# The last 25 slots of a software-pipelined kernel, rewritten as a closing program for each engine

## The chip, the cores and the metric

The kernel runs on one core of a Trainium2 chip. The core has TensorE (PE in the rows), VectorE (DVE), ScalarE (ACT), GpSimd (POOL) and SyncE (SP), which here only issues transfers. The metric is the device time of one execution in microseconds; the span is the part of it from the first to the last instruction.

## The reference

```python
def _L0_attn_ref(query, key_param, Wq, bq, Wk, bk, Wv, bv, Wo, bo):
    ...
    scores = jnp.einsum('blhe,bshe->bhls', queries, keys)
    A = sparsemax(scale * scores)
    out = jnp.einsum('bhls,bshd->blhd', A, values)
    out = jnp.transpose(out, (0, 2, 1, 3)).reshape(B, L, H * D)
    return out @ Wo + bo
def _L0_ffn_ref(x, Win, bin_, W1, b1, W2, b2, Wout, bout):
    s = jnp.einsum('btd,dm->btm', x, Win) + bin_
    h = jax.nn.relu(s[..., None] * W1 + b1)
    g = jnp.einsum('btmh,mh->btm', h, W2) + b2
    out = jnp.einsum('btm,md->btd', g, Wout) + bout
    return out
x = L0_attn_query
x = _layernorm(x + _L0_attn_ref(x, ...), axis=-1)
x = _layernorm(x + _L0_ffn_ref(x, ...), axis=-1)
```

x is 16 x 1024 x 512 in fp32. The attention has 16 heads and 32 key patterns; the feed-forward has 64 units s, each with 16 hinges relu(s * w1 + b1), summed with the weights W2.

## The kernel before, in words

The 16384 rows are 128 tiles of 128 rows (TILES). All engines run through one list of slots, 176 of them, numbered from 0. In slot n each engine does one step for several tiles at once, and the constants LAG_... say how many slots behind a tile is at each step: scores of tile n-1, the sparsemax in the next slots, the large product with the folded value and output weights of tile n-23 (LAG_WO, L663, four fp32 products of 512 columns), its residual with row sums on VectorE (n-24, L954), the first layernorm's result y (n-25), the transposes of y and the 64 units s (n-26, L648 and L677), the copy of s on ScalarE (n-27, L796), and so on. The scores of the last tile fall in slot 128 and the last large product in slot 150. From there to slot 175 the loop runs only the later steps.

The hinges are worked on in groups of four tiles (GROUP), 512 columns at a time. The 128 partitions hold the 64 units twice, once for each half of the 16 hinges, so a group takes 8 hinge steps: ScalarE writes one (L783) into one of two buffers `hinge`, and VectorE adds it times w2c into `acc` (L1111, then seven times L1115), two in a slot. When a group is full, its two halves are folded in the **group slot** (`split_lead`, slots 34, 38, ... 150 and then a last one in 156): ScalarE copies the upper half to `both` (L805), GpSimd adds the lower half (L512), ScalarE rounds the sum to `split` and `second` (L842, L843), and GpSimd writes the rest of the sum beside it (L514). Then TensorE can form the feed-forward output of the four tiles, one in a slot (n-34, L697 and L698; called f below). VectorE adds it to y (n-35, L954 again), and the second layernorm follows.

A layernorm is spread over three engines. GpSimd turns the row sum into two small numbers (L466, L468), ScalarE takes the sum of squares (L771), GpSimd makes the reciprocal root and the shift (L476, L481, L484), and one instruction on 128x512 applies them: for y in L831 or L1018, for the output in L825 or L1012. `vector_finishes` says who does that: ScalarE before slot 128 and VectorE from slot 128 on, together with the copy of the transposed y from PSUM (L855 on ScalarE, L1001 on VectorE). SyncE stores the output from the ring o_sb of four places (L423).

Every engine works strictly in the order of its code, and all waits are on semaphores. So an instruction that waits holds back everything behind it on its engine:

```python
                if lead is not None and lead != LAST:

                    pool.wait_ge(s_upper, lead // GROUP + 1)
                    nc.gpsimd.tensor_tensor(both[0:M, :], acc[0:M, :], both[0:M, :], ALU.add).then_inc(s_both, 1)
                    pool.wait_ge(s_hi, lead // GROUP + 1)
                    nc.gpsimd.tensor_tensor(split[M:P, :], both[0:M, :], split[0:M, :].bitcast(F32),
                                            ALU.subtract).then_inc(s_lo, 1)
```

## Time and profile before

| what | value |
|---|---|
| median of 3 runs | 1354.32 us (1354.13 to 1356.15) |
| the profiled execution | 1352.76 us, of which the span is 1351.0 us |
| mean granted TensorE clock | 0.967 |
| PE, DVE, ACT, POOL busy | 1251.9, 1138.9, 1053.6, 703.2 us |
| slots 128 to 150 in the trace | 1152.1 us to about 1294 us |
| after that, to the end of the span | about 57 us |

The granted clock is 1.00 at 2.4 GHz and 0.50 at 1.2 GHz. In a timeline row stand the start, the length, the engine, the line, the operation and its tiles; in square brackets how long the engine was idle ahead of it and what it waited for. Matmuls in fp32 are recorded as two entries each, so four products read x8. An instruction's successor can start some 0.08 us before its own end.

### The profile page before, as it was taken

The page shows a single profiled execution, that of the slowest core. Times are in us where ns is not written, and L with a number is a line of the kernel's source. Part 1 is how long each engine was busy: PE and PEld are TensorE (multiplying, and loading weights), DVE is VectorE, ACT ScalarE, POOL GpSimd, SP SyncE. Part 2 cuts the span into 40 slices and gives each one's busy share as a digit, 9 for nine tenths or more (in the row PEclk, how much of TensorE's full clock was granted, in tenths as well). Part 3 has the DMA queues.
Part 4 walks back from the last instruction along what each step waited for, and adds up shares of the span by engine and source line. Part 5 has one row for each costly group of instructions (what it writes and reads, how often), then busy time and mean ns, then how long its engine had stood idle before and what let it go on. Part 6 is the DMA issues. An engine that isn't in the chain of part 4 may idle for free. (4 is left out here: it accounts for less than half of the span.)

```text
span 1351.0 us, 25359 instructions
## 1 busy us (share of the span) xinstructions
PE 1251.9 (93%) x5838; PEld 867.3 (64%) x5838; DVE 1138.9 (84%) x4573; ACT 1053.6 (78%) x2269; POOL 703.2 (52%) x1674
## 2 busy tenths in 40 slices
PE   7982889999999999999999999999999999899962
PEld 6651666766776776776776776776776777555541
DVE  3977788889999999999999999999998999876764
ACT  2671756688898888899898898888899899666654
POOL 1330333345565555555556555555555556567663
PEclk9995999999999999999999999999999999999975
DMA  6380786555655655655655655655655655668733
GB/s 189 93 210 26 193 231 208 179 171 182 215 189 197 219 192 191 219 193 191 218 192 193 218 192 192 219 196 189 217 195 190 217 196 182 210 231 296 251 94 70
DMA packets 92374, 258.36 MB, mean 191 GB/s; under 512 B 16259, under 2 KB 16259, under 8 KB 75814
## 3 DMA queue, kind: packets, MB, share of 16 engines
q1 hardware_dynamic: 92198, 256.52, 58.7%
q14 instruction: 128, 1.05, 0.3%
q8 instruction: 48, 0.79, 0.2%
HBM read 206.13 MB, written 50.33 MB: 190 GB/s over the span
## 5 line engine op out<-in xcount | busy, mean ns | idle before, releaser
L663 PE MATMUL bank<-G_sb,pT 128*128 128x512 f32 x1024 | 461.1, 593 | 1.9 <-ACT pT L758 1.8
L663 PEld LDWEIGHTS bank<-G_sb,pT 128*128 128x128 f32 x1024 | 185.0, 191 | 185.9 <-issue 183.4
L1077 DVE MAX8 top<-bank 128x8 f32<-128x32 f32 x2048 | 212.3, 179 | 44.5 <-issue 44.5
L466 POOL TENSOR_TENSOR shift_sq<-sum,per_row_sq 128x1 f32<-128x1 f32 x256 | 96.0, 375 | 265.7 <-DVE y_sb L954 263.2
L771 ACT ACTIVATE unread<-y_sb,shift_sq 128x512 bf16<-128x512 f32 x256 | 183.9, 718 | 51.8 <-POOL minus_mean L468 51.7
L1115 DVE SCALAR_TENSOR_TENSOR acc<-hinge,w2c,acc 128x512 f32<-128x512 f32 x224 | 167.4, 748 | 61.7 <-ACT hinge L783 58.3
L783 ACT ACTIVATE hinge<-s_sb,b1c,w1c 128x512 f32<-128x512 f32 x256 | 205.8, 807 | 0.2
L588 PE MATMUL bank<-A_hi,xT_hi 128*128 128x512 f32 x512 | 204.0, 399 | 0.0
L590 PE MATMUL bank<-A_hi,xT_lo 128*128 128x512 f32 x512 | 203.9, 398 | 0.0
L589 PE MATMUL bank<-A_lo,xT_hi 128*128 128x512 f32 x512 | 203.7, 398 | 0.0
L481 POOL TENSOR_TENSOR rstd<-ve,minus_half 128x1 f32<-128x1 f32 x256 | 164.8, 644 | 43.1 <-POOL ve L476 42.8
L677 PEld LDWEIGHTS bank<-yT,Win_sb 128*128 128x128 f32 x1024 | 136.2, 195 | 73.7 <-issue 55.2
L849 ACT CAST xT_hi<-bank 128x512 fp32r<-128x512 f32 x128 | 74.7, 583 | 133.0 <-PE bank L637 133.0
L954 DVE SCALAR_TENSOR_TENSOR y_sb<-bank,y_sb 128x512 f32<-128x512 f32 x256 | 169.2, 661 | 0.0
L677 PE MATMUL bank<-yT,Win_sb 128*128 128x128 f32 x1024 | 138.6, 279 | 11.1 <-DVE yT L1001 11.1
L491 POOL TENSOR_TENSOR side<-side 128x256 bf16<-128x256 bf16 x128 | 85.5, 668 | 117.6 <-ACT side L866 117.6
L589 PEld LDWEIGHTS bank<-A_lo,xT_hi 128*128 128x128 f32 x512 | 97.1, 190 | 23.7
L590 PEld LDWEIGHTS bank<-A_hi,xT_lo 128*128 128x128 f32 x512 | 97.0, 189 | 23.8
L588 PEld LDWEIGHTS bank<-A_hi,xT_hi 128*128 128x128 f32 x512 | 97.1, 190 | 22.3 <-issue 0.5
L602 PE MATMUL bank<-ident,u_sb 128*128 128x128 f32 x512 | 78.9, 278 | 32.8 <-DVEq L1070 26.2
L758 ACT ACTIVATE pT<-bank 128x512 f32<-128x512 f32 x128 | 76.7, 599 | 39.8 <-PE bank L602 36.8
L1040 DVE TENSOR_TENSOR xT_lo<-bank,xT_hi 128x512 fp32r<-128x512 f32 x128 | 87.6, 685 | 21.1 <-ACT xT_hi L849 20.9
(133 smaller groups left out, 2421.9 us busy)
## 6 DMA issues: line engine op xcount, KB each, us to landing
G_sb<-G_of_heads SPq DMA_DIRECT2D x128, 1024.0 KB, 5.4
x_sb<-in_L_attn_query_dram SPq DMA_DIRECT2D x128, 256.0 KB, 4.7
y_sb<-in_L_attn_query_dram SPq DMA_DIRECT2D x256, 128.0 KB, 5.4
out_dram<-o_sb SPq DMA_DIRECT2D x256, 128.0 KB, 4.7
G_of_heads<-y_sb SPq DMA_DIRECT2D x64, 256.0 KB, 3.8
y_sb<-in_L_attn_Wk_dram SPq DMA_DIRECT2D x1, 1024.0 KB, 5.7
y_sb<-in_L_attn_Wq_dram SPq DMA_DIRECT2D x1, 1024.0 KB, 8.2
y_sb<-in_L_attn_Wv_dram SPq DMA_DIRECT2D x1, 1024.0 KB
```

The lines of the kernel that those rows point to most:

```text
L466: nc.gpsimd.tensor_tensor(shift_sq[:, par:par + 1], total[:, par:par + 1], per_row_sq[:], ALU.mult).then_inc(s_mean, 1)
L481: nc.gpsimd.tensor_tensor(rstd[:, par:par + 1], ve[:], minus_half[:], ALU.pow).then_inc(s_rstd, 1)
L588: nc.tensor.matmul(ps[:], hi[:, c, :], w_hi[:, c, :], start=start and c == 0, stop=False)
L589: nc.tensor.matmul(ps[:], hi[:, c, :], w_lo[:, c, :], start=False, stop=False)
L590: mm = nc.tensor.matmul(ps[:], lo[:, c, :], w_hi[:, c, :], start=False, stop=(c == C - 1))
L663: mm = nc.tensor.matmul(o_ps[i % 2][:], pT[:, bass.ds(pair_place(turn, i) + (i % H * C + c) * P, P)], G_sb[:, i % GR, c, :], start=(c == 0 ...
L677: mm = nc.tensor.matmul(s_ps[:, 0:P], Win_sb[:, c, :], yT[:, c, :], start=(c == 0), stop=(c == C - 1))
L771: nc.scalar.activation(unread[:], y_sb[:, i % YR, :], ACT.Square, bias=shift_sq[:, i % 2:i % 2 + 1], scale=1.0 / D ** 0.5, accum_out=var[: ...
L783: nc.scalar.activation(hinge[:, k % HR, :], s_sb[:, g % 2, :], ACT.Relu, bias=b1c[:, k:k + 1], scale=w1c[:, k:k + 1]).then_inc(s_hinge, 1)
L954: nc.vector.scalar_tensor_tensor(rows, ps[:], 0.0, other, ALU.add, ALU.add, accum_out=total).then_inc(s_rows, 1)
L1077: mx = nc.vector.max(top8[:, h, :], z_ps[i % 2][:, h * S:(h + 1) * S])
L1115: nc.vector.scalar_tensor_tensor(acc[:], hinge[:, k % HR, :], w2c[:, k:k + 1], acc[:], ALU.mult, ALU.add).then_inc(s_acc, 1)
```

## The change

The loop now ends after slot 150 (SLOTS is 151). What the 25 remaining slots did is written out by hand at the end of each engine's program:

- Hinge sums of the last two groups (tiles 120 to 123 and 124 to 127, called group 0 and 1 of the closing). VectorE adds only the even hinges into acc. The odd ones go to TensorE: `unit_sum` multiplies a hinge buffer by `w2_rows`, a 128x64 matrix that holds w2 and folds both halves, and `add_acc` brings acc in by a product with `both_halves`. The sums are in a PSUM bank, where ScalarE rounds them (`round_sum`) and VectorE takes the rest (`rest_of_sum`). GpSimd builds the two matrices in slot 144.
- Second layernorm of the last 12 tiles, 116 to 127: row sums and squares have columns of their own (`sum_end`, `var_end`), GpSimd handles two tiles with each small instruction (`mean_pair`, `norm_pair`), the squares of tiles 116 to 121 are on VectorE and those of 122 to 127 on ScalarE.
- Output of tiles 115 to 127: written in place in y_sb and stored from there, 7 of them by GpSimd, 3 by VectorE, 3 by ScalarE.
- The f of tiles 116 on rotates over four PSUM banks (`f_place`).

Two things change inside the loop as well. In the group slots for tiles 100, 104, 108, 112 and 116 (slots 134 to 150, ON_VECTOR) the add and the subtract on 64x512 move from GpSimd to VectorE. And the copy of the transposed y stays on ScalarE to the end, while y and the output move to VectorE from slot 131 on instead of 128.

```diff
-        SLOTS = TILES + FILL * UNROLL
-
-        def slots(eng, slot):
-
-
-            for turn in range(SLOTS // UNROLL):
-                for j in range(UNROLL):
-                    slot(turn, j)
+        SLOTS = TILES + LAG_WO
...
-        def vector_finishes(turn):
-
-
-            return isinstance(turn, int) and turn >= TILES // UNROLL
+        def vector_finishes(turn, j):
+
+
+            return turn * UNROLL + j >= TILES + FILL
...
+        ENDING = (LAST - GROUP, LAST)
+        FIRST_END = SLOTS - LAG_NORM2
+        ON_VECTOR = LAST - 6 * GROUP
...
+            if i >= LAST - 2 * GROUP:
+                return (f_ps, uT_ps, o_ps[0], o_ps[1])[i % GROUP]
...
+        FINAL_P = list(range(FIRST_END - 1, FIRST_END + 6))
+        FINAL_V = [FIRST_END + 6, FIRST_END + 8, FIRST_END + 10]
+        FINAL_A = [FIRST_END + 7, FIRST_END + 9, FIRST_END + 11]
+        SQUARE_V = list(range(FIRST_END, FIRST_END + 6))
+        SQUARE_A = list(range(FIRST_END + 6, TILES))
...
-            if 0 <= lead < LAST:
-                return [(lead, 2 * q + half)]
-            if lead == LAST and 2 * q < GROUP:
-                return [(lead, 4 * q + 2 * half), (lead, 4 * q + 2 * half + 1)]
-            return []
+            return [(lead, 2 * q + half)] if 0 <= lead < ENDING[0] else []
...
+                if base + j == TILES + UNROLL:
+
+                    nc.gpsimd.tensor_tensor(both_halves[:], ident[:, 0:M], ident[:, M:P], ALU.add).then_inc(s_halves, 1)
+                    pool.wait_ge(s_halves, 1)
+                    pool.wait_ge(s_p, TILES)
+                    nc.gpsimd.tensor_tensor(w2_rows, both_halves[:].unsqueeze(1).broadcast_to([P, KH, M]),
+                                            w2c[:].unsqueeze(2).broadcast_to([P, KH, M]), ALU.mult).then_inc(s_w2rows, 1)
                 lead = split_lead(turn, j)
-                if lead is not None and lead != LAST:
+                if lead is not None and lead < ON_VECTOR:
...
+            def mean_pair(n):
+
+                cols = pair_cols(n)
+                pool.wait_ge(s_r2, FIRST_END + 2 * n + 2)
+                nc.gpsimd.tensor_tensor(shift_sq_end[:, cols], sum_end[:, cols], per_row_sq[:].broadcast_to([P, 2]),
+                                        ALU.mult).then_inc(s_mean_end, 1)
...
+            norm1(TILES - 2)
+            mean(TILES, (TILES - 1) % 2, s_r1, sum1, s_mean1, minus_mean1, shift_sq1, s_shift1)
+            i = FIRST_END - 1
+            norm(i + 1, i % 2, s_var2, var2, s_ve2, ve2, s_mean2, minus_mean2, s_rstd2, rstd2, s_shift2, shift2, s_final)
+            norm1(TILES - 1)
+            final_end(nc.gpsimd, FINAL_P[0], s_final_p)
+            mean_pair(0)
+            mean_pair(1)
+            norm_pair(0)
+            for i in FINAL_P[1:3]:
+                final_end(nc.gpsimd, i, s_final_p)
+            norm_pair(1)
+            for i in FINAL_P[3:5]:
+                final_end(nc.gpsimd, i, s_final_p)
+            mean_pair(2)
+            mean_pair(3)
+            norm_pair(2)
+            for i in FINAL_P[5:7]:
+                final_end(nc.gpsimd, i, s_final_p)
+            norm_pair(3)
+            mean_pair(4)
+            mean_pair(5)
+            norm_pair(4)
+            norm_pair(5)
...
+                if LAST - 2 * GROUP + 2 <= base + i < ENDING[0]:
+                    pe.wait_ge(s_r1, TILES - GROUP + i % GROUP + 1)
+                elif base + i >= ENDING[0]:
+                    pe.wait_ge(s_r2, base + i - 3)
...
+            def unit_sum(g, k):
+
+                pe.wait_ge(s_hinge, SUMS + g * KH + k + 1)
+                nc.tensor.matmul(end_sums(g), w2_rows[:, k, :], hinge[:, k % HR, :], start=(k == 1),
+                                 stop=(k == KH - 1)).then_inc(s_kmm, 1)
+
+            def add_acc(g):
+
+                pe.wait_ge(s_acc, SUMS + (g + 1) * KH // 2)
+                nc.tensor.matmul(end_sums(g), both_halves[:], acc[:], start=False, stop=False)
...
+            end = FIRST_END
+            units_t(*at(TILES - 3, LAG_YT))
+            feed_forward(*at(end + 1, LAG_OUT))
+            units(*at(TILES - 3, LAG_YT))
+            units_t(*at(TILES - 2, LAG_YT))
+            pe.wait_ge(s_u1, TILES)
+            pe.wait_ge(s_halves, 1)
+            pe.wait_ge(s_w2rows, 1)
+            unit_sum(0, 1)
+            units(*at(TILES - 2, LAG_YT))
+            feed_forward(*at(end + 2, LAG_OUT))
+            unit_sum(0, 3)
+            units_t(*at(TILES - 1, LAG_YT))
+            feed_forward(*at(end + 3, LAG_OUT))
+            unit_sum(0, 5)
+            units(*at(TILES - 1, LAG_YT))
+            add_acc(0)
+            unit_sum(0, 7)
+            unit_sum(1, 1)
+            feed_forward(*at(end + 4, LAG_OUT))
+            feed_forward(*at(end + 5, LAG_OUT))
+            unit_sum(1, 3)
+            feed_forward(*at(end + 6, LAG_OUT))
+            unit_sum(1, 5)
+            feed_forward(*at(end + 7, LAG_OUT))
+            add_acc(1)
+            unit_sum(1, 7)
+            for i in range(LAST, TILES):
+                feed_forward(*at(i, LAG_OUT))
...
+            def end_hinge(g, k):
+
+                n = g * KH + k
+                if k == 0:
+                    act.wait_ge(s_sc, ENDING[g] + GROUP)
+                if k % HR == 0:
+                    act.wait_ge(s_acc, SUMS + n // HR if n >= HR else SUMS - 1)
+                elif n >= HR:
+                    act.wait_ge(s_kmm, n // HR)
+                else:
+                    act.wait_ge(s_acc, SUMS)
+                nc.scalar.activation(hinge[:, k % HR, :], s_sb[:, ENDING[g] // GROUP % 2, :], ACT.Relu,
...
+            def round_sum(g):
+
+                parts, high = end_split[g]
+                act.wait_ge(s_kmm, (g + 1) * KH // 2)
+                act.wait_ge(s_ones, 2)
+                nc.scalar.copy(parts[0:M, :], end_sums(g)).then_inc(s_hi, 1)
+                act.wait_ge(s_hi, ENDING[g] // GROUP + 1)
+                nc.scalar.copy(high[0:M, :], parts[0:M, :].bitcast(F32)).then_inc(s_high, 1)
...
+            copy_s(LAST)
+            end_hinge(0, 0)
+            copy_yT(TILES - 3)
+            end_hinge(0, 1)
+            end_hinge(0, 2)
+            square(0, TILES - 1 + LAG_NORM1, LAG_NORM1, s_mean1, s_var2, FIRST_END, shift_sq1, s_ve1, var1, s_var1)
+            copy_s(LAST + 1)
+            end_hinge(0, 3)
+            copy_yT(TILES - 2)
+            end_hinge(0, 4)
+            copy_s(LAST + 2)
+            end_hinge(0, 5)
+            copy_yT(TILES - 1)
+            end_hinge(0, 6)
+            copy_s(LAST + 3)
+            end_hinge(0, 7)
+            end_hinge(1, 0)
+            end_hinge(1, 1)
+            round_sum(0)
+            for k in range(2, KH):
+                end_hinge(1, k)
+            round_sum(1)
+            for i in SQUARE_A:
+                square_end(i)
+            for i in FINAL_A:
+                final_end(act, i, s_final_a)
...
-                if split_lead(turn, j) == LAST:
-                    dve.wait_ge(s_upper, TILES // GROUP)
+                late = split_lead(turn, j)
+                if late is not None and late >= ON_VECTOR:
+                    dve.wait_ge(s_upper, late // GROUP + 1)
                     nc.vector.tensor_tensor(both[0:M, :], acc[0:M, :], both[0:M, :], ALU.add).then_inc(s_both, 1)
-                    dve.wait_ge(s_hi, TILES // GROUP)
-                    nc.vector.tensor_tensor(last_split[M:P, :], both[0:M, :], last_split[0:M, :].bitcast(F32),
-                                            ALU.subtract).then_inc(s_lo, 1)
-                if in_range(turn, j, LAG_YT) and vector_finishes(turn):
-                    i = j - LAG_YT
-                    dve.wait_ge(s_yT, base + i + 1)
-                    dve.wait_ge(s_s, base + i)
-                    dve.wait_ge(s_yTc, base + i)
-                    nc.vector.tensor_copy(yT[:].rearrange("p c n -> p (c n)"), ys_ps[:]).then_inc(s_yTc, 1)
...
+            end, last = FIRST_END, TILES - 1
+            residual_end(end)
+            make_y(last - 1)
+            residual(last + 1, o_ps[last % 2], s_o, y_sb[:, last % YR, :], s_xr[last % YR], 32 * (TILES // YR),
+                     y_sb[:, last % YR, :], sum1[:, last % 2:last % 2 + 1], s_mean1, s_r1)
+            add_hinge(0, 0)
+            residual_end(end + 1)
+            add_hinge(0, 2)
+            make_y(last)
+            add_hinge(0, 4)
+            residual_end(end + 2)
+            add_hinge(0, 6)
+            residual_end(end + 3)
+            rest_of_sum(0)
+            add_hinge(1, 0)
+            square_end(end)
+            square_end(end + 1)
+            add_hinge(1, 2)
+            square_end(end + 2)
+            square_end(end + 3)
+            residual_end(end + 4)
+            add_hinge(1, 4)
+            residual_end(end + 5)
+            residual_end(end + 6)
+            add_hinge(1, 6)
+            residual_end(end + 7)
+            rest_of_sum(1)
+            square_end(end + 4)
+            square_end(end + 5)
+            for i in range(LAST, TILES):
+                residual_end(i)
+            for i in FINAL_V:
+                final_end(dve, i, s_final_v)
```

On VectorE, the last group slot of the loop (slot 150) and the start of what follows, before; `both` is the folded sum, `yT` the transposed y:

```order
L954 SCALAR_TENSOR_TENSOR y_sb,sum<-bank,y_sb 128x512
L1001 COPY yT<-bank 128x512
L954 SCALAR_TENSOR_TENSOR y_sb,sum<-bank,y_sb 128x512
L1012 TENSOR_SCALAR o_sb<-y_sb,rstd,shift 128x512
L1018 TENSOR_SCALAR y_sb<-y_sb,rstd,shift 128x512
L1111 TENSOR_SCALAR acc<-hinge,w2c,b2c 128x512
L1115 SCALAR_TENSOR_TENSOR acc<-hinge,w2c,acc 128x512
```

The same place now, and the first rows of the closing:

```order
L1189 SCALAR_TENSOR_TENSOR y_sb,sum<-bank,y_sb 128x512
L1235 TENSOR_TENSOR both<-acc,both 64x512
L1189 SCALAR_TENSOR_TENSOR y_sb,sum<-bank,y_sb 128x512
L1246 TENSOR_SCALAR o_sb<-y_sb,rstd,shift 128x512
L1250 TENSOR_TENSOR split<-both,split 64x512
L1196 TENSOR_SCALAR y_sb<-y_sb,rstd,shift 128x512
L1358 SCALAR_TENSOR_TENSOR y_sb,sum_end<-bank,y_sb 128x512
L1196 TENSOR_SCALAR y_sb<-y_sb,rstd,shift 128x512
L1189 SCALAR_TENSOR_TENSOR y_sb,sum<-bank,y_sb 128x512
L1379 TENSOR_SCALAR acc<-hinge,w2c,b2c 128x512
```

The copy of yT is gone from VectorE, `both` and `split` have come in, and the first hinge of tiles 120 to 123 stands two residuals and one y later than before.

On TensorE, the closing from the first units to the first f of tiles 120 to 123, now (L731 are the units, L716 the transposes, L754 and L755 an f, L861 `unit_sum`, L867 `add_acc`):

```order
L731 MATMUL bank<-yT,Win_sb 128x128 x4
L754 MATMUL bank<-Wout_hi,split 128x512
L755 MATMUL bank<-Wout_lo,second 128x512
L861 MATMUL bank<-hinge,u_sb 64x512
L716 MATMUL bank<-ident,y_sb 128x128 x4
L754 MATMUL bank<-Wout_hi,split 128x512
L755 MATMUL bank<-Wout_lo,second 128x512
L861 MATMUL bank<-hinge,u_sb 64x512
L731 MATMUL bank<-yT,Win_sb 128x128 x4
L867 MATMUL bank<-acc,both_halves 64x512
L861 MATMUL bank<-hinge,u_sb 64x512 x2
L754 MATMUL bank<-Wout_hi,A_hi 128x512
```

The rows L861 and L867, fp32 products of 512 columns, are new; there are ten of them in the closing, and the units and transposes of the last tiles stand between them.

## Rows read from the trace of the kernel before

**Rows 1.** The page: span, and two lines of its 40 slices.
```profile
span 1351.0 us, 25359 instructions
...
PE   7982889999999999999999999999999999899962
...
PEclk9995999999999999999999999999999999999975
```
**Rows 2.** Busy by stretch: us, PE, PEld, DVE, ACT, POOL busy (instructions), clock, DMA, GB/s.
```profile
1204.00:1225.00 21.00, 21.00 (x89) 12.72 (x88) 15.27 (x35) 13.33 (x28) 14.44 (x38) 1.00 0.78 254
1225.00:1248.00 23.00, 21.38 (x89) 12.59 (x88) 16.94 (x36) 13.87 (x31) 16.32 (x41) 1.00 0.88 300
...
1294.00:1316.00 22.00, 11.63 (x44) 9.13 (x44) 13.27 (x27) 13.29 (x28) 12.80 (x32) 0.68 0.24 54
1316.00:1330.00 14.00, 4.24 (x8) 2.16 (x8) 9.86 (x18) 9.45 (x16) 4.99 (x13) 0.50 0.09 20
1330.00:1351.00 21.00, 5.14 (x9) 2.01 (x8) 6.93 (x19) 5.38 (x14) 8.19 (x33) 0.50 0.45 100
```
**Rows 3.** Timeline of PE, slots 129 to 135: its waits.
```profile
1163.99 1.16 PE L677 MATMUL bank<-yT,Win_sb 128*128 128x128 f32 x8 [2.60 <-DVE yT L1001]
...
1165.35 0.77 PE L697 MATMUL bank<-Wout_hi,split 128*128 128x512 f32 x1
...
1179.61 1.16 PE L677 MATMUL bank<-yT,Win_sb 128*128 128x128 f32 x8 [1.02 <-DVE yT L1001]
...
1183.59 0.19 PE L628 MATMUL bank<-differs,ones_col 128*1 128x4 f32 x2 [2.36 <-DVE differs L970]
...
1203.57 3.70 PE L663 MATMUL bank<-G_sb,pT 128*128 128x512 f32 x8 [1.75 <-ACT pT L758]
```
**Rows 4.** Timeline of PE: large products of slots 139, 143, 147, and slot 150's f.
```profile
1224.57 3.60 PE L663 MATMUL bank<-G_sb,pT 128*128 128x512 f32 x8
...
1247.89 3.60 PE L663 MATMUL bank<-G_sb,pT 128*128 128x512 f32 x8
...
1271.14 3.60 PE L663 MATMUL bank<-G_sb,pT 128*128 128x512 f32 x8
...
1293.97 0.50 PE L697 MATMUL bank<-Wout_hi,split 128*128 128x512 f32 x1 [1.10 <-POOL split L514]
```
**Rows 5.** Timelines of ACT, POOL and DVE in the group slot 150.
```profile
1289.65 0.62 ACT L805 COPY both<-acc 64x512 f32<-64x512 f32 x1 [0.57 <-DVE acc L1115]
...
1290.67 1.26 POOL L512 TENSOR_TENSOR both<-acc,both 64x512 f32<-64x512 f32 x1
...
1292.66 1.26 POOL L514 TENSOR_TENSOR split<-both,split 64x512 fp32r<-64x512 f32 x1 [0.73 <-ACT split L842]
...
1295.91 0.54 DVE L1111 TENSOR_SCALAR acc<-hinge,w2c,b2c 128x512 f32<-128x512 f32 x1 [3.24 <-ACT hinge L783]
```
**Rows 6.** Groups by line and shape, 1204 to 1294 us: busy us, mean ns | idle before.
```profile
L783 ACT ACTIVATE hinge<-s_sb,b1c,w1c 128x512 f32<-128x512 f32 x30 | 24.0, 799 | 0.0
...
L954 DVE SCALAR_TENSOR_TENSOR y_sb<-bank,y_sb 128x512 f32<-128x512 f32 x32 | 21.8, 680 | 0.0
L771 ACT ACTIVATE unread<-y_sb,shift_sq 128x512 bf16<-128x512 f32 x30 | 21.5, 718 | 25.0 <-POOL minus_mean L468 25.0
...
L1115 DVE SCALAR_TENSOR_TENSOR acc<-hinge,w2c,acc 128x512 f32<-128x512 f32 x27 | 20.4, 754 | 13.1 <-ACT hinge L783 13.1
```
**Rows 7.** Timelines of PE, ACT, POOL and DVE after slot 150.
```profile
1299.34 2.08 PE L677 MATMUL bank<-yT,Win_sb 128*128 128x128 f32 x8 [4.20 <-DVE yT L1001]
...
1344.76 0.72 ACT L771 ACTIVATE unread<-y_sb,shift_sq 128x512 bf16<-128x512 f32 x1 [1.70 <-POOL minus_mean L468]
...
1346.08 0.55 POOL L481 TENSOR_TENSOR rstd<-ve,minus_half 128x1 f32<-128x1 f32 x1 [0.17 <-POOL ve L476]
...
1347.05 0.55 DVE L1012 TENSOR_SCALAR o_sb<-y_sb,rstd,shift 128x512 f32<-128x512 f32 x1 [1.97 <-POOL shift L484]
```
**Rows 8.** Two lines by source: ns least/median/most, first to last start.
```profile
L1033 DVE TENSOR_TENSOR u_sb<-u_raw,step x108: 691/692/1726, 196.3 to 1172.7; 128x512 f32<-128x512 f32 x108
...
L507 POOL MEMSET A_lo<- x1: 529/529/529, 1158.7 to 1158.7; 128x512 f32 x1
```

261 lines of the change are left out of this document (187 added, 74 removed).

## The prediction

> **What bounds the kernel now.** I read the page's slices first [rows 1]: PE is at 9 tenths or more almost everywhere, and falls only in the last two slices, where its clock falls too. The change lies in the last 200 us, so I read the windows there next [rows 2]. From 1204 to 1225 us PE is busy for all 21.00 us, four slots long. In 1225 to 1248 it is busy 21.38 of 23. From 1294 us on nobody is bound by his own work: in the last 21 us PE has 5.14 us, DVE 6.93, ACT 5.38 and POOL 8.19. That is a chain of waits. So there are three stretches with three limits, and I cost each by itself: A, slots 128 to 134; B, slots 135 to 150; C, all behind it.
>
> In A the timeline of PE shows what it waits for [rows 3]: 2.60, 1.02, 2.36 and 1.75 us, together 7.73, each time for VectorE or ScalarE. After the longest, the first matmul of an f takes 0.77 us, against 0.50 at 1293.97 [rows 3, 4]: the clock had fallen to 1.2 GHz for a moment.
>
> In B the large products of slots 135, 139, 143 and 147 start at 1203.57, 1224.57, 1247.89 and 1271.14 [rows 3, 4]. Four slots take 21.00 us (5.25 a slot, PE's own work), then 23.32 and 23.25. The difference is the group slot: ScalarE copies half of acc, GpSimd adds 64x512 in 1.26 us but only from 1290.67 on, since its norms stand ahead, ScalarE rounds, GpSimd subtracts in 1.26 us [rows 5]. f then waits 1.10 us for POOL [rows 4], and GpSimd's means are late, so ScalarE's squares are, so VectorE stands still for 3.24 us before the next hinge [rows 5].
>
> In C, from the f at 1293.97 to 1351.0, are 57.0 us. Here every tile goes around once: f, residual, mean, square, norm, output. In the last rounds a square starts at 1344.76 and its output at 1347.05, 2.29 us later, with 1.70 us of idle ScalarE ahead of the square [rows 7].
>
> **The change, part by part.**
>
> *A, slots 128 to 134.* In slots 128 to 130 VectorE loses the copy of yT, y and the output, three instructions of some 0.6 us a slot (as other 128x512 ones: 0.68 in L954, 0.55 in L1012 [rows 6, 7]). I count 0.6 + 0.5 + 0.5 = 1.6, and 0.7 of waiting once. VectorE is then early by 3.6 us at the end of slot 129. PE's wait of 2.60 for yT goes away, since ScalarE, which now copies it, is idle in that slot; with it goes about 1.3 us of slow clock, 3.9 in all. In slot 130 the new copy stands behind the rounding of the group and PE waits for it, +1.3. In slot 131 the wait of 1.02 goes, and in 132 VectorE's comparison is early, so that about half of the 2.36 goes (-1.2). In slot 134 the split is on VectorE, so ScalarE comes to its last pT sooner: half of 1.75 (-0.9). Sum: -3.9 + 1.3 - 1.0 - 1.2 - 0.9 = -5.7; I take -5.2. Bounds: -3 (only the 2.60 goes) to -7.7 (all four waits).
>
> *B, slots 135 to 150.* If every slot were PE's 5.25 us, the group waits give back 2.3, 2.25 and, from slot 147 to slot 150's f, 22.83 - (3 x 5.25 + 3.44 + 0.81) = 2.8. Here 3.44 is the row's 3.60 for four large products without the last one's tail of 0.16 [rows 4], and 0.81 is what then remains of 5.25 for the units of a tile beside an f (0.55) and transposes (0.45). Sum -7.4. Is there a ring that takes more than 5.25? One goes: residual on VectorE 0.68, means on POOL about 0.5, square 0.72, hinge 0.80, square 0.72, hinge 0.80, add on VectorE 0.75 [rows 6]: 4.97, and less with the overlaps. In a group slot the copy of acc, VectorE's add, two roundings and the copy of yT stand ahead of the squares: 0.6 each, some 6.6 us for that slot and 21.0 for four. That is what PE takes too, so nothing is left over there; hence -6.7 rather than -7.4. On POOL, slot 144 gets the making of w2_rows, a two-input product over 512 elements for which L512 is the nearest row (1.26 us, 512 elements), and a small one, 1.5 in all; ScalarE's squares wait for it, and PE has about half a slot in hand: +0.7. B is -6.0, bounds -3 to -7.4. Here VectorE has the group add and subtract, 1.4 us in a group slot, and is 3.24 us idle there now, so they cost nothing; without that cover they would cost their 1.4.
>
> So slot 150's f starts at 1293.97 - 11.2 = 1282.8.
>
> *C, the closing.* What is removed: 25 rounds of the loop, one mean and norm per tile in turn, and 8 of the 16 adds of a hinge (0.75 each). What is new: ten fp32 products of 512 columns on PE. Four of them are 3.60 us in the loop with the tail, 0.86 each without it [rows 4]. At 1.2 GHz they are 1.72, by the units, x8 in 2.08 us there [rows 7] against half of that in the loop. PE's list in C is 3 units and transposes (1.25 each), 12 f (0.55), ten products: 19 us at 2.4 GHz, and 37 at 1.2. DVE has some 21 us, ACT 23, POOL 17 to 23. Nobody is the bound at the high clock, so I follow the chain, with time 0 at slot 150's f, in pairs for the two clocks:
> - f 0.6, residual 0.7, y of tile 126 0.5, residual of 127 0.6, mean 0.5, ScalarE behind a hinge 1.1, square 0.7, norm and y of 127 1.6: 6.3 (6.7).
> - Meanwhile PE does the units of 126, f, one unit_sum, and the transposes of 127; they end at 8.7 (11.3). Then f, unit_sum, copy of yT, units of 127: 11.1 (15.7).
> - VectorE's fourth add, add_acc, hinge 7, unit_sum: 13.1 (19.1). Rounding, and its rest on VectorE, two hops: 15.1 (21.2).
> - Group 1: three even hinges with VectorE's squares and residuals in between, four unit_sums and three f on PE: 24.0 (32.5). Round and rest: 25.4 (33.9).
> - Two squares on VectorE 1.4, norm of a pair 1.3, two outputs on POOL 1.8, next norm 1.3, means: ScalarE starts the squares of 124 to 127 at 31.4 (39.9). Four squares 2.9, the last norm 1.3, an output 0.8: 36.6 (45.0).
> - From the last output to the end, as now, 1351.0 - 1347.6 = 3.4 [rows 7]: 40.0 (48.4).
>
> So C is -17.0 at full clock throughout and -8.6 at half throughout. In the stretch before, the clock fell once PE had stood idle for 4.20 us, and did not come back while PE was busy for some 80% [rows 2, 7]. My chain has PE idle for under 2 us at a time, but busy for only 19 of 26 us, so I expect it to fall for part of the closing: 44, plus 1 for what follows, 45. C is -12.0.
>
> The outputs of 512 columns on POOL are not in the trace. From below a memset of 512 columns, 0.53 us [rows 8], from above a two-input op of as many, 1.26 [rows 5]; with one tensor input it is nearest the middle, 0.9. Seven of them, four in the chain. The row of L1033 on VectorE, 0.69 us as a rule and 1.73 at most [rows 8], says that a VectorE instruction with two SBUF inputs is at times held, and POOL's folds run then. VectorE's hinge adds and squares have two SBUF inputs and meet POOL's outputs, each up to 1 us: I take one us in all; the upper bound is 5.
>
> The Trainium skill (SBUF — State Buffer, the section on two separate sides) makes a rule of this: such a VectorE instruction and a GpSimd one exclude each other for their whole length. It speaks against GpSimd's outputs; by it every meeting costs up to a full instruction, and the sum would be near that upper bound, 1334 in place of 1330 for the profiled execution. The same notes (GPSIMD Engine Reference, elementwise cycle accounting) have 769 ns for 512 elements in the best case, as an estimate 0.13 us less a tile than I took.
>
> **Sum.** -5.2 - 6.0 - 12.0 = -23.2, from the profiled execution's 1352.76: 1329.6. The median of the runs is 1.56 above that one, so I state 1331.
>
> **The rivals.**
> 1. The closing at full clock and POOL's outputs unhindered: C is -17.0, so 1324.6, 1326 beside the median. For it: the chain leaves no long idle time on PE. Against: PE's busy share there is below the loop's.
> 2. PE at 1.2 GHz through the closing, where ten products of 1.72 make it the bound, and VectorE and POOL hold each other: C is -8.6 + 5 = -3.6; 1352.76 - 14.8 = 1338.0, or 1339.5. By the exclusion rule of the skill named above this is where the time would go.
> 3. Slower than before. One mechanism: the copy of yT on ScalarE closes a ring, since it waits for PE's transposes, which wait for VectorE's y, and the squares and hinges now stand behind it. The ring is 4.97 + 0.6 by the rows above if nothing overlaps, 5.6 a slot, and the slots of B take 5.8 on average now. To eat the 17 to 18 us of C and A over 20 slots it would have to be 0.9 above today's, 6.7 a slot; at 7 the time would be near 1360. Against it: ScalarE is idle 25.0 us before its squares in 90 us [rows 6], more than the 9 us that 15 copies take.
> 4. The closing is shorter on paper only, each pair waiting for its second tile: then A and B alone remain and C is 0, 1341.6, or 1343.
>
> **How the numbers follow.** My forecast, a clock that falls for part of the closing (1327 to 1336), 0.55. Rival 1, 0.18. Rival 2, 0.19. Rival 4, 0.05, rival 3 or something like it 0.03. The range 1323 to 1341 takes in rivals 1 and 2, with A and B at their bounds partly. About 0.2% (2.7 us) is what a measurement of this kernel can tell from no change: faster 0.95, within it 0.02, slower 0.03.
>
> **What the profile after would show.** The f of slot 150 at 1281 to 1285 us. Large products of slots 139, 143 and 147 21 to 21.5 us apart, without a wait of f for POOL; PE without the 2.60 us idle time. In the closing, PE's clock between 0.5 and 1; unit_sum at 0.9 or 1.7 us; POOL's outputs at 0.8 to 1.3; from that f to the end 40 to 49 us. Wrong would be: groups still 23 us apart (another ring), a unit_sum that waits for its hinge for several us, or POOL's outputs at over 2 us.

## The result, and the profile after

The changed kernel takes 1333.66 us (median of 4 runs, 1332.68 to 1335.14), the kernel before 1354.22 in the same comparison: a ratio of 0.9856, 95% interval 0.9844 to 0.9868, 20.6 us less. A second comparison, beside the first three experiments, gives 1333.92 against 1355.61 (0.9846, 0.9833 to 0.9860). The forecast was 1331, with a range of 1323 to 1341.

The profiled execution has a span of 1333.0 us; it was the one that took 1335.14. The page, as in [rows 1]:

```profile
span 1333.0 us, 25293 instructions
...
PE   6982889999999999999999999999999999989993
...
PEclk9995989999999999999999999999999999999998
```

The second-last slice went from 6 to 9 tenths busy, and the clock is at full speed up to the last slice. In [rows 1] it had fallen to 7 and 5. The windows of the last 175 us show the same by stretch (columns as in [rows 2]):

```profile
1158.00:1200.00 42.00, 37.45 (x167) 23.14 (x165) 26.65 (x63) 34.21 (x74) 23.77 (x66) 0.96 0.70 230
...
1223.00:1245.00 22.00, 21.57 (x90) 12.94 (x89) 15.19 (x34) 16.27 (x35) 12.46 (x39) 1.00 0.86 278
...
1293.00:1303.00 10.00, 8.88 (x34) 3.76 (x34) 4.29 (x8) 6.66 (x11) 1.95 (x5) 1.00 0.12 26
1303.00:1313.00 10.00, 6.60 (x16) 2.11 (x16) 8.02 (x20) 4.89 (x7) 7.05 (x14) 1.00 0.25 56
1313.00:1323.00 10.00, 2.11 (x8) 1.42 (x8) 5.20 (x14) 4.88 (x13) 5.33 (x15) 0.85 0.58 128
1323.00:1333.00 10.00, 0.00 (x0) 0.00 (x0) 1.09 (x2) 3.00 (x5) 1.27 (x5) 0.50 0.60 132
```

The clock column is the thing to see: 1.00 while the closing's products run, although PE is busy for only 66% of the ten microseconds from 1303 on. It falls only behind PE's last product, which ends at 1316.1, and there it costs nothing.

PE's waits and large products, the counterpart of [rows 3, 4]:

```profile
1165.21 0.66 PE L766 MATMUL bank<-ident,u_sb 128*128 128x128 f32 x4 [1.04 <-ACT pT L931]
...
1170.55 1.16 PE L731 MATMUL bank<-yT,Win_sb 128*128 128x128 f32 x8 [1.25 <-ACT yT L961]
...
1179.96 0.19 PE L792 MATMUL bank<-differs,ones_col 128*1 128x4 f32 x2 [2.12 <-DVE differs L1212]
...
1180.97 4.89 PE L818 MATMUL bank<-G_sb,pT 128*128 128x512 f32 x8
...
1200.59 3.70 PE L818 MATMUL bank<-G_sb,pT 128*128 128x512 f32 x8 [0.74 <-ACT pT L931]
...
1222.67 3.70 PE L818 MATMUL bank<-G_sb,pT 128*128 128x512 f32 x8 [0.79 <-DMA G_sb<-G_of_heads]
...
1250.54 3.70 PE L818 MATMUL bank<-G_sb,pT 128*128 128x512 f32 x8 [0.78 <-DMA G_sb<-G_of_heads]
...
1286.96 0.48 PE L754 MATMUL bank<-Wout_hi,split 128*128 128x512 f32 x1
```

The 2.60 us wait for yT is gone, and with it the 1.02. In its place stand 1.04 for pT and the forecast 1.25 for a copy of yT that ScalarE makes late. The 2.36 is now 2.12, the 1.75 is 0.74. In slots 135 to 150 no wait for GpSimd is left; what ends PE's waits there is the transfer of G (the folded value and output weights that each large product reads, 1 MB a tile), four times, 2.42 us together. Before, none of PE's waits in these slots ended with it. The groups of four slots from 135, 139 and 143 take 22.08, 21.70 and 22.63 us; the forecast had 21 to 21.5, and another ring as the sign that it was wrong. The f of slot 150 has no wait at all (1.10 in [rows 4]).

Counted from slot 128's large product, which starts at 1152.13 before and 1152.67 after, the three stretches are, in microseconds:

| | before | after | forecast change | measured change |
|---|---|---|---|---|
| A, to slot 135's large product | 51.44 | 47.92 | -5.2 | -3.5 |
| B, from there to slot 150's f | 90.40 | 86.37 | -6.0 | -4.0 |
| C, the closing | 57.03 | 46.04 | -12.0 | -11.0 |

With the 0.54 by which this execution reached slot 128 later that makes the 18.0 between the two spans. The medians lie 20.6 apart.

Last, the end of the closing, as in [rows 7], from the timelines of ScalarE, DVE and SP's queue:

```profile
1320.24 0.72 ACT L1101 ACTIVATE unread<-y_sb,shift_sq_end 128x512 bf16<-128x512 f32 x1 [4.72 <-POOL minus_mean_end L606]
...
1323.68 2.32 ACT L307 ACTIVATE y_sb<-y_sb,shift_end,rstd_end 128x512 f32<-128x512 f32 x3
```
```profile
1325.19 0.55 DVE L309 TENSOR_SCALAR y_sb<-y_sb,rstd_end,shift_end 128x512 f32<-128x512 f32 x1 [1.27 <-POOL shift_end L625]
```
```profile
1324.51 6.24 SPq L473 DMA_DIRECT2D out_dram<-y_sb  x10
```

ScalarE waits 4.72 us before it can square tile 124, though VectorE had the residuals of 124 and 125 done 3.4 us earlier, at 1316.85: GpSimd makes the outputs of 120 and 121 and a norm first. The last output ends at 1326.0. The end is 7.0 us after it, where it was 3.4 before. SP issues the stores of the last five tiles one by one, 0.62 us each, up to 1330.75. It had stood at tile 123's, whose output waited for ScalarE's squares.

So three questions were open. Is B now held by G's transfers? Is the tail held by SP's issues or by the data? What does each part of the change give?

### The profile page after: what moved, and what is told of

It reads as the page before. It is cut to its first block and busy times, and to the rows that moved or that the text cites. A ratio compares the mean times of both kernels' runs of the same rounds, so it can differ in the third digit from the quotient of the medians.

```text
span 1333.0 us, 25293 instructions
## 1 busy us (share of the span) xinstructions
PE 1251.6 (94%) x5858; PEld 863.7 (65%) x5858; DVE 1120.3 (84%) x4545; ACT 1066.7 (80%) x2290; POOL 680.9 (51%) x1642
## 3 DMA queue, kind: packets, MB, share of 16 engines
q14 instruction: 128, 1.04, 0.3%
## 5 line engine op out<-in xcount | busy, mean ns | idle before, releaser
L1349 DVE SCALAR_TENSOR_TENSOR acc<-hinge,w2c,acc 128x512 f32<-128x512 f32 x210 | 156.4, 745 | 63.0 <-ACT hinge L971 61.7
L971 ACT ACTIVATE hinge<-s_sb,b1c,w1c 128x512 f32<-128x512 f32 x240 | 193.3, 808 | 0.0
L944 ACT ACTIVATE unread<-y_sb,shift_sq 128x512 bf16<-128x512 f32 x244 | 175.0, 717 | 6.9 <-POOL minus_mean L518 6.6
L731 PEld LDWEIGHTS bank<-yT,Win_sb 128*128 128x128 f32 x1024 | 134.1, 191 | 65.3 <-issue 58.6
L531 POOL TENSOR_TENSOR rstd<-ve,minus_half 128x1 f32<-128x1 f32 x244 | 153.8, 630 | 41.0 <-POOL ve L526 40.7
L1189 DVE SCALAR_TENSOR_TENSOR y_sb<-bank,y_sb 128x512 f32<-128x512 f32 x244 | 160.1, 660 | 1.8 <-PE bank L755 1.3
L731 PE MATMUL bank<-yT,Win_sb 128*128 128x128 f32 x1024 | 135.4, 275 | 3.0 <-ACT yT L961 3.0
```

Of the source, the lines that this page charges most:

```text
L531: nc.gpsimd.tensor_tensor(rstd[:, par:par + 1], ve[:], minus_half[:], ALU.pow).then_inc(s_rstd, 1)
L731: mm = nc.tensor.matmul(s_ps[:, 0:P], Win_sb[:, c, :], yT[:, c, :], start=(c == 0), stop=(c == C - 1))
L944: nc.scalar.activation(unread[:], y_sb[:, i % YR, :], ACT.Square, bias=shift_sq[:, i % 2:i % 2 + 1], scale=1.0 / D ** 0.5, accum_out=var[: ...
L971: nc.scalar.activation(hinge[:, k % HR, :], s_sb[:, g % 2, :], ACT.Relu, bias=b1c[:, k:k + 1], scale=w1c[:, k:k + 1]).then_inc(s_hinge, 1)
L1189: nc.vector.scalar_tensor_tensor(rows, ps[:], 0.0, other, ALU.add, ALU.add, accum_out=total).then_inc(s_rows, 1)
L1349: nc.vector.scalar_tensor_tensor(acc[:], hinge[:, k % HR, :], w2c[:, k:k + 1], acc[:], ALU.mult, ALU.add).then_inc(s_acc, 1)
```

## The experiments

Each was timed in 5 rounds beside the kernel before; ratios are to it. The changed kernel itself ran beside the first three experiments only. The intervals of most single experiments overlap with its 0.9844 to 0.9868 and 0.9833 to 0.9860, so their gains of one to three microseconds are not shown by the times alone. Because single profiles reach slot 128 at anything from 1149.4 to 1154.0 us, I compare stretches A, B and C, and they don't all repeat equally well:

- C of the closing as changed is 46.04, 46.05, 46.06 and 46.18 us in four executions of three programs, all with the group folds on VectorE. With the folds on GpSimd it is longer, 47.06, 47.63 and 49.25 (below).
- B of six executions with the same loop runs from 85.35 to 87.62 us, 86.37 on average. The spread is that of PE's waits for G, 1.27 to 3.70 us; without them B is 83.9 to 84.5.
- A has two values, 46.2 to 46.3 and 47.9 to 48.0 us (next part).

### The changed kernel again

> The changed kernel itself, as the yardstick for the three kernels that run beside it. All theories: ratio to the kernel before 0.985 to 0.987, about 1333.5 us, the f of slot 150 at some 1287 us in the profile and the closing 46.0 us.

Measured: 1333.92 us, 0.9846 (0.9833 to 0.9860). A 46.26, B 87.14, C 46.05. C repeats to 0.01 us. A is 1.66 shorter, and the difference is one thing: the large product behind the wait for differs takes 3.60 us here and not 4.89, and the transposes just ahead of it are shorter too. TensorE's clock had fallen there in the one execution and not in the other (called a slow product below).

### The group's add and subtract back on GpSimd

```diff
-        ON_VECTOR = LAST - 6 * GROUP
+        ON_VECTOR = LAST
```

> The changed kernel with the group's add and subtract back on GpSimd in the loop (ON_VECTOR = LAST); the closing is untouched. Theory 1 (stretch B gained because the group slot's stall for GpSimd went, and now the transfers of G hold it at 21.7 to 22.6 us per four slots): the group waits come back, f of a group waits about 1 us for GpSimd, four slots take 23.2 us, the f of slot 150 comes 3 to 4 us later, the time is 1336.5 to 1337.5. Rival a (the transfers of G set the pace of B in any case, and the gain in B came from the rest of the loop's change): four slots stay at 21.7 to 22.6 us, the time stays within 1 us of the changed kernel's. The closing takes 46 us in either.

Measured: 1336.70 us, 0.9865 (0.9849 to 0.9880), 2.8 us above the changed kernel beside it. B is 88.85, with 22.67 and 23.47 us for the four slots from 139 and from 143. The waits for G shrink to 0.36 us, and these come instead:

```profile
1264.56 1.16 PE L731 MATMUL bank<-yT,Win_sb 128*128 128x128 f32 x8 [2.24 <-ACT yT L961]
```

Theory 1 holds in size. Its wait stands elsewhere than I wrote: not f waits for GpSimd, but the units wait for a yT copy that is queued on ScalarE behind the rounding, and the rounding waits for GpSimd. The move to VectorE is worth about 2.8 us of the time. In the profile it shows in all three stretches: A is 47.30 without a slow product, 1.0 more than 46.26, and C is 47.06, 1.0 more, though the closing is the same program: its first unit_sum starts 4.6 us behind slot 150's f instead of 3.4. B without its waits for G is 88.5, against 83.9 to 84.5 in the changed kernel, so as an estimate the move frees some 4 us there and the transfers of G take about 2 of them back.

### The closing programs alone

```diff
-            return turn * UNROLL + j >= TILES + FILL
+            return turn * UNROLL + j >= TILES
-                if in_range(turn, j, LAG_YT):
+                if in_range(turn, j, LAG_YT) and not vector_finishes(turn, j):
                     copy_yT(base + j - LAG_YT)
```

VectorE copies yT in slots 128 to 150 again, where it did before, and ON_VECTOR is LAST.

> The closing programs alone: in the loop the yT copy, y and the output go back to VectorE from slot 128 on and the group's add and subtract back to GpSimd, as in the kernel before. Theory 1 (A gave 3 us, B 4, the closing 11): the f of slot 150 comes at 1293 to 1294.5 us, the closing takes 46 to 47 us, the time is 1340 to 1341.5, 7 us more than the changed kernel. Rival b (the loop's change is worth little by itself, the closing gives nearly all): less than 3 us more than the changed kernel, below 1336.5. Rival c (the closing only works since ScalarE and VectorE enter it early): the closing takes over 48 us and the time is above 1343.

Measured: 1346.76 us, 0.9938 (0.9924 to 0.9951). None of the three theories had all of this: it is 12.8 us above the changed kernel, where theory 1 had 7, and with the time of rival c the closing is not over 48 us. A is 53.27, B 92.55, C 47.63. The closing is nearly all there, 9.4 of 11.0 us. But the loop is longer than in the kernel before. In A it is chance: slots 128 to 134 are the program of the kernel before, and this execution has a slow product of 5.29 us behind the wait for differs, which the kernel before and the other execution of these slots (A 51.55, below) don't have. B is 2.15 us longer, most of it in the group that holds slot 144, 25.04 us against 23.25 in the kernel before; the waits for G are 1.90. The closing needs w2_rows, and GpSimd makes it there:

```profile
1258.47 0.32 POOL L561 TENSOR_TENSOR both_halves<-ident 128x64 f32<-128x64 f32 x1
1258.87 1.04 POOL L564 TENSOR_TENSOR u_sb<-both_halves,w2c 128x512 f32<-128x512 f32 x1
```

So the parts are not simply added: the closing's part costs something in the loop, and the loop's part takes it back. Against the changed kernel, which has a slow product too, A is 5.4 us longer here, B 6.2 and C 1.6. The loop's part without the closing was not run.

### Two tiles' stores from ScalarE's queue

```diff
+            for i in (125, 127):
+                act.wait_ge(s_final_a, FINAL_A.index(i) + 1)
+                for half in (1, 0):
+                    nc.scalar.dma_start(out_rows[i // H, i % H, half],
...
```

> The changed kernel with the stores of tiles 125 and 127 issued by ScalarE behind its last output, those of 123, 124 and 126 still by SP. In the changed kernel SP issues the last ten stores one after another in 6.24 us, from 1324.51 on, and the end comes 7.0 us after the last output. Theory 1 (the tail is the serial issue of stores, 0.62 us each): SP is through after six, at 1328.2, ScalarE after four behind 1326.0, at 1328.5, and the time falls by 2.2 to 2.6 us, to about 1331. Rival d (the tail is the transfer of the data and its landing): the time stays within 0.5 us of the changed kernel's, since the same bytes go out behind the same outputs.

SP leaves these two out. Measured: 1332.18 us, 0.9833 (0.9820 to 0.9846); the medians differ by 1.7, with overlapping intervals, the profiles' C by 1.2 (44.83). The two queues:

```profile
1321.45 3.84 SPq L475 DMA_DIRECT2D out_dram<-y_sb  x6
```
```profile
1322.16 3.05 ACTq L1135 DMA_DIRECT2D out_dram<-y_sb  x4
```

Both are through at 1325.2 us, 2.3 after the last output, as against 4.7 before: the issue got 2.4 shorter, as expected. The end still comes 3.4 us behind that, not 2.25. ScalarE's stores land after 3.5 us by the DMA view and the six of SP beside them after 2.9, where SP's alone took 2.4. So issue was the limit for half of the expected gain, then the landing takes over. Both theories are half right.

### All hinge adds on VectorE

```diff
-                nc.tensor.matmul(end_sums(g), both_halves[:], acc[:], start=False, stop=False)
+                nc.tensor.matmul(end_sums(g), both_halves[:], acc[:], start=True, stop=True).then_inc(s_kmm, 1)
```

The unit_sums go, and add_hinge is called for odd k too.

> The changed kernel with all eight hinge adds of each of the last two groups on VectorE again; TensorE only joins the halves of acc in one product a group. Seven to eight adds of 0.75 us come into VectorE's program, half of them on the chain from the f of slot 150 to the second rest. Theory 1 (the hinge sums set the chain in the middle of the closing, and sharing them is a main part of its gain): the closing takes 3 to 5 us more, 49 to 51 us, the time is 3 to 5 us above the changed kernel's, ratio 0.987 to 0.989. Rival e (VectorE's 12 us of idle time in the closing take the adds for nothing): within 1 us of the changed kernel's 0.985.

Measured: 1336.83 us, 0.9872 (0.9854 to 0.9890). C is 48.94, 2.9 more. The adds are only part of it. This is what else happened on PE:

```profile
1298.43 1.07 PE L867 MATMUL bank<-acc,both_halves 128*64 128x512 f32 x2 [1.95 <-DVE acc L1370]
1300.89 0.73 PE L754 MATMUL bank<-Wout_hi,A_hi 128*128 128x512 f32 x1 [1.39 <-DVE A_hi L1377]
1301.42 0.63 PE L755 MATMUL bank<-Wout_lo,A_lo 128*128 128x512 f32 x1
...
1312.70 1.97 PE L867 MATMUL bank<-acc,both_halves 128*64 128x512 f32 x2 [8.14 <-DVE acc L1370]
```

In the changed kernel a product of an f takes 0.40 us and the second add_acc 1.07. Here the clock has already fallen to 1.2 GHz at 1300.9, behind waits of 2.73, 0.56, 1.95 and 1.39 us in twelve, and it is low again behind the 8.14. The granted clock is 0.81 from 1296 to 1304 us, 0.71 from 1304 to 1312 and 0.50 from there. The unit_sums are work that VectorE needn't do, and they also keep PE's idle times below 1.6 us in the closing's middle, where the clock stays at 2.4 GHz. How the 2.9 us divide between the adds and the clock, this run doesn't separate.

### Statistics one tile at a time

```diff
+                for m in (2 * n, 2 * n + 1):
+                    cols = slice(m, m + 1)
```

around the bodies of mean_pair and norm_pair, each with its own wait.

> The changed kernel with mean and norm of the last twelve tiles one tile at a time, 1 column an instruction in place of 2, in the same places of GpSimd's program. That is 30 small instructions of 0.19 to 0.69 us more, some 9 us of GpSimd's time, about half of it while somebody waits for it. Theory 1 (pairs save GpSimd's time, and GpSimd's program is what the last rounds wait for): the closing takes 2 to 4 us more, ratio 0.9865 to 0.988. Rival f (a single tile's norm starts a square earlier, and this pays for the added instructions): within 1 us of the changed kernel's.

Measured: 1334.27 us, 0.9854 (0.9838 to 0.9870), which is no difference that this comparison can tell. In the profile the last output ends 41.9 us behind slot 150's f, 2.8 later than the 39.0 of the changed kernel, and C is 47.96, 1.9 longer; B was short in this execution (86.03). By this one profile the pairs save about 2 us of the closing, at the bottom of what I expected, and SP's queue hides a third of what they give; the times don't confirm it.

### The means of 124 and 125 earlier on GpSimd

```diff
             norm_pair(2)
+            mean_pair(4)
+            norm_pair(3)
+            mean_pair(5)
             for i in FINAL_P[5:7]:
                 final_end(nc.gpsimd, i, s_final_p)
-            norm_pair(3)
-            mean_pair(4)
-            mean_pair(5)
```

> The changed kernel with one change of order on GpSimd: after the norm of 120 and 121 come the means of 124 and 125, the norm of 122 and 123, the means of 126 and 127 and only then the outputs of 120 and 121. ScalarE's wait of 4.72 us before the square of 124 gets shorter by 2.0 to 2.5 us, since the residuals of 124 and 125 are done at 29.9 and 30.4 us behind the f of slot 150 and the square starts at 33.3. Theory 1 (SP's serial issue of stores sets the end): the last output comes 2 us sooner, but the stores of 120 to 127, 16 of 0.62 us, now start later than before, so the time stays within 0.7 us of the changed kernel's. Rival g (the chain of squares and norms sets the end): the time falls by 2.0 to 2.5 us, ratio 0.983.

Measured: 1332.93 us, 0.9841 (0.9827 to 0.9854); C 45.38, 0.7 less.

```profile
1316.24 0.72 ACT L1101 ACTIVATE unread<-y_sb,shift_sq_end 128x512 bf16<-128x512 f32 x1 [1.84 <-POOL minus_mean_end L606]
```
```profile
1318.72 10.25 SPq L473 DMA_DIRECT2D out_dram<-y_sb  x16
```

(The residuals that I put at 29.9 and 30.4 us are done at 29.3 and 29.9.) The wait falls from 4.72 to 1.84, the last output ends 37.2 us behind slot 150's f instead of 39.0, and the end moves by 0.7 only. SP now has sixteen stores in a row, 0.64 us each, from 1318.72 to 1328.97. Theory 1 holds. This is the clearest evidence on the tail: the chain gave 1.8 us and the queue of stores kept 1.1 of them.

### Four places for G

```diff
+        def G_place(i):
...
+            n = i % GR4 - GR
+            return pT[:, n * C * D:(n + 1) * C * D].rearrange("p (c n) -> p c n", c=C)
```

Tiles 112 to 127 take turns over the two places of G_sb and two in the half of pT that is free by then; each load waits for the product four tiles back.

> The changed kernel with four places in place of two for the G of the last sixteen tiles (two of them in the half of pT that is free then), loaded up to three tiles ahead; the same bytes. TensorE waited 2.4 to 3.2 us for G in slots 135 to 150. Theory 1 (a transfer lands too late only since it can't start before the place is free): the waits for G go, the slots are 5.25 us, from slot 135's large product to slot 150's f 84 to 84.5 us instead of 86.4 to 87.1, the time falls by 2.0 to 3.0 us. Rival h (the transfers are at the limit of what the DMA engines move, 0.87 to 0.91 busy): the waits are still there, merely later, and the time stays within 0.7 us.

Measured: 1332.63 us, 0.9834 (0.9821 to 0.9848). PE waits for G no more; B is 83.71, 2.7 less than the average of the six executions with two places and 1.6 less than the shortest, and the first two groups take 21.02 and 20.90 us. The DMA views of the changed kernel, from 1199 to 1283 us, then of this one, from 1201 to 1285, each starting a little before slot 135's large product (busy tenths of the DMA engines; what was moved):

```profile
DMA  8918989969898598699797998938989789998999
...
DMA packets 7207, 24.02 MB, mean 286 GB/s; under 512 B 1244, under 2 KB 1244, under 8 KB 5288
```
```profile
DMA  9999999999999988989989899998988998050500
...
DMA packets 7266, 24.02 MB, mean 286 GB/s; under 512 B 1264, under 2 KB 1264, under 8 KB 5360
```

The same 24 MB go through sooner, and the last slices of the second line are nearly empty. I read the digits 1, 5 and 3 in the first line as moments in which no place is free to load into. The limit in B was a missing place. The engines' bandwidth was not it.

### The copy of yT alone back on VectorE

```diff
-                if in_range(turn, j, LAG_YT):
+                if in_range(turn, j, LAG_YT) and base + j < TILES:
                     copy_yT(base + j - LAG_YT)
+                if in_range(turn, j, LAG_YT) and base + j >= TILES:
...
+                    nc.vector.tensor_copy(yT[:].rearrange("p c n -> p (c n)"), ys_ps[:]).then_inc(s_yTc, 1)
```

> The changed kernel with the copy of yT alone back on VectorE in slots 128 to 150. Closing programs alone stood 12.8 us above the changed kernel, the same with the early outputs and the yT copy on ScalarE (group folds still on GpSimd) only 2.8, so these two are worth 10 us together. Theory 1 (in A it is the 2.60 us wait for yT that goes with the copy, 4 us with the slow clock; in B VectorE's 0.6 us a slot): A 51 to 53 us in place of 46.3 to 47.9, B 1 to 3 us more, the time 6 to 9 us above the changed kernel's, ratio 0.990 to 0.992. Rival i (it is y and the output, three slots later on VectorE, that take the load off, and the copy hides in VectorE's idle time): within 2 us of the changed kernel's.

y, the outputs and the group's add stay as changed. Measured: 1337.22 us, 0.9870 (0.9854 to 0.9885), 2 to 3 us above the changed kernel, as the two comparisons have it. A is 49.52 (1.6 more than the 47.92, both with a slow product), B 87.64 with 3.04 of waits for G, so 84.6 without them, as good as the changed kernel's 83.9 to 84.5, and C 46.06. The copy's price stands in A. That is less than theory 1 wanted and a bit more than the rival. The wait for yT in slot 129 is back at 1.28 us, not 2.60. So most of the 10 us between the closing alone and the kernel with folds on GpSimd should come with y and the outputs starting on VectorE in slot 131 instead of 128. That is a subtraction: no run here moves only those.

### w2_rows at the start of the closing

The combined kernel of the next part, and the closing programs alone, each with both_halves and w2_rows made behind the closing's first norm, in place of slot 144:

```diff
-                if base + j == TILES + UNROLL:
-
-                    nc.gpsimd.tensor_tensor(both_halves[:], ident[:, 0:M], ident[:, M:P], ALU.add).then_inc(s_halves, 1)
...
             norm1(TILES - 2)
+            nc.gpsimd.tensor_tensor(both_halves[:], ident[:, 0:M], ident[:, M:P], ALU.add).then_inc(s_halves, 1)
...
```

> The combined kernel with both_halves and w2_rows made by GpSimd at the start of the closing, in the 2.1 to 2.7 us in which it waits for the residual of 127, in place of slot 144. They take 0.32 and 1.04 us. Theory 1 (in slot 144 they delay the means, squares and the next slots by about 0.7 us): four slots from 143 to 147 take 20.9 us in place of 21.6, the closing is unchanged, the time 0.5 to 0.8 us less. Rival (slot 144 has slack for them): no change in B; and if the mean of 127 or the first unit_sum comes late, the closing is up to 1 us longer.

Measured: 1326.67 us, 0.9796 (0.9783 to 0.9809). The four slots from 143 take 20.90 us in place of 21.62, B is 82.88 against the combined kernel's 83.70, and C 43.12 against 42.98. The 0.7 us for slot 144 is shown. The medians lie 2.6 us apart; the rest of that no stretch accounts for.

> The closing programs alone, as before, with both_halves and w2_rows made at the start of the closing in place of slot 144. There GpSimd still has the group's add and subtract and f waited 1.71 us for it in that group; four slots from 143 to 147 took 25.04 us, in the kernel before 23.25. Theory 1 (making them costs the loop its whole 1.4 us and more where GpSimd sets the group slot's end): the four slots take 23.3 us again, and the time is 1.5 to 2 us less than 1346.8, ratio 0.992 to 0.9925. Rival (the longer group came from the transfers of G, 1.31 us of wait just before it): still 24.5 to 25 us, and the time within 0.7 us of the closing programs alone.

Measured: 1346.18 us, 0.9945 (0.9932 to 0.9959), not told apart from the 0.9938 of the closing alone. The four slots take 23.88, 1.2 less, and f waits 1.52 us for GpSimd there as it waited 1.71. B is 91.07. The group is still 0.6 longer than the 23.25 of the kernel before, for which I have no cause, but the rival, G's transfers, falls: PE has no wait for G inside either group (the 1.31 us stood before slot 143). C is 49.25, 1.6 more, and that is not w2_rows: the mean of 127 starts 4.1 us behind slot 150's f here and 4.0 in the closing alone. It is TensorE's clock. The first unit_sum, here and in the closing alone:

```profile
1300.52 1.97 PE L859 MATMUL bank<-hinge,u_sb 128*64 128x512 f32 x2
```
```profile
1302.61 1.07 PE L861 MATMUL bank<-hinge,u_sb 128*64 128x512 f32 x2
```

The units and transposes ahead of it take 1.47 and 1.06 us for 1.16 and 0.60, with a granted clock of 0.62 from 1298 to 1302 us, so the unit_sum is through 7.8 us behind the f instead of 6.2: the whole 1.6. Both executions have PE waits of 1.52 and 1.98 us just ahead, and only this one lost the clock. So making w2_rows costs the loop about 1.2 us here, and moving it gives that back; in this execution the slow clock took it again.

### The gains together

Four places for G and the two tiles' stores on ScalarE's queue, as above, the means first, and the outputs of 120, 121 and 123 on VectorE:

```diff
-        FINAL_P = list(range(FIRST_END - 1, FIRST_END + 6))
-        FINAL_V = [FIRST_END + 6, FIRST_END + 8, FIRST_END + 10]
-        FINAL_A = [FIRST_END + 7, FIRST_END + 9, FIRST_END + 11]
+        FINAL_P = [115, 116, 117, 118, 119]
+        FINAL_V = [120, 121, 122, 123, 124, 126]
+        FINAL_A = [125, 127]
```

> What the runs before pointed to, put together: four places for G, the stores of 125 and 127 issued by ScalarE, GpSimd's means of 124 and 125 ahead of its norm of 122 and 123, and the outputs of 120 and 121 moved from GpSimd to VectorE, with that of 123. If the three gains add (G 2.8 us from slot 135 to slot 150's f, the order 1.8 us at the last output, the stores 1.2 us or more behind it, since SP's issue no longer holds what the order gives): 83.7 us in B and 41 to 42.5 us in the closing, the time 5 to 7 us below the changed kernel's, 1327 to 1328.5, ratio 0.980. If the DMA engines are the limit at the end (0.5 to 0.9 busy there): the closing 43.5 to 44.5 us and the ratio 0.982.

Measured: 1329.23 us, 0.9815 (0.9802 to 0.9828). B is 83.70, C 42.98, between the two expectations: the last output ends 36.9 us behind slot 150's f, and the end is 6.1 after it. With w2_rows moved it is the 1326.67 above, 0.9796, whose interval lies wholly below both of the changed kernel's: 7 to 8 us less.

## Why the prediction was right, and where it was not

**A.** The forecast's steps held in kind: the wait of 2.60 went, so did the 1.02, and the new wait for yT in slot 130 came at 1.25 us for the 1.3 written. The sum of -5.2 is exact in the executions without a slow product (46.26, so -5.2) and 1.7 too large in the others (47.92). Slot by slot it was -3.3 in slot 129 (forecast -3.9), +0.7 in slot 130 (+1.3), -1.5 in 131 (-2.2 for both waits) and -1.0 in 134 (-0.9). Of nine executions whose slots 128 to 134 hold the same program, five have the slow product, four don't. Two terms failed. The wait for differs, which I had halved, shrank from 2.36 to 2.12 only, and in five of nine the clock fell behind it. And the "about 1.3 us of slow clock" behind the wait of 2.60 was worth next to nothing: in the closing alone with w2_rows moved these slots are the program of the kernel before, with the same 2.60 and the clock at 1.00 throughout, and A is 51.55, no shorter than 51.44. PE waits 1.10 and 1.03 us for pT there instead of 0.20 and 0.46. That the sum comes out exact is in part luck.

**B.** The forecast was -6.0 with VectorE in the group's fold and +0.7 for w2_rows. With G out of the way B is 83.71 (-6.7), and 82.88 without w2_rows in slot 144 (-7.5). So the +0.7 for w2_rows is confirmed, and the 0.7 that I kept back for the group slots' longer ring, -6.7 for -7.4, was not needed: every group ran at PE's pace. Measured was -4.0 in the one profile and -3.3 in the other. The missing 2 to 3 us are G's transfers. My question was "is there a ring that takes more than 5.25?", and I listed only rings of compute engines. The ring of a place for G is product, then load, then product again. In [rows 2] the DMA share was already 0.88, and the trace of the kernel before has G's loads land in 5.7 to 8.3 us from 1204 us on, 6.5 in the median; two slots of 5.25 less a product of 3.6 leave 6.9. The median fits and the slowest don't. That there would be waits was to be read from the profile, their size was not.

**C.** -12.0 against -11.0, so the size is right, but by luck: two of its steps failed in opposite directions. The clock was to fall for part of the closing, at a cost of some 4 us. It stayed at 2.4 GHz to PE's last product, with PE never idle for more than 1.6 us. The kernel with all adds on VectorE, and the closing alone with w2_rows moved, show the fall that I feared, behind waits of up to 2.73 and 1.98 us; so it was nearer than C's four equal values suggest. In its place came 6 us that the chain at full clock doesn't have. Its milestones, behind slot 150's f, as forecast at full clock and as measured:

| | forecast | measured |
|---|---|---|
| y of 127 done | 6.3 | 6.9 |
| units of 127 | 11.1 | 11.8 |
| unit_sum(0, 7) | 13.1 | 14.0 |
| round and rest | 15.1 | 16.0 |
| group 1's sums | 24.0 | 25.7 |
| squares of 124 start | 31.4 | 33.3 |
| last output | 36.6 | 39.0 |
| the end | 40.0 | 46.0 |

The chain is 2.4 us too long in small amounts; the largest between two milestones are 0.8, up to group 1's sums, and 0.6, up to y of 127, of which 0.4 are that y beside an output of GpSimd (0.93 us for 0.54). The other 3.6 come from the term "as now, 3.4". Before, outputs came 2.51 us apart, and SP had only the two stores of 127 left when its output ended at 1347.60: 1.1 us of issue and 2.3 from there to the end. Now the last five tiles' outputs are ready within 2.1 us, and SP issues ten stores of 0.62 us, through 4.75 us behind the last output; the rest is 2.25 as before. A term taken over from the old schedule was wrong in the new one.

**GpSimd's outputs** take 0.77 us, for my 0.9. The last two of them, from its timeline:

```profile
1317.13 1.52 POOL L309 TENSOR_SCALAR y_sb<-y_sb,rstd_end,shift_end 128x512 f32<-128x512 f32 x2
```

The Trainium skill (GPSIMD Engine Reference, elementwise cycle accounting) has 769 ns for 512 elements in the best case, and the trace agrees within 1%: six of the seven outputs take 0.77 to 0.78 us. With it the sum would have been 0.5 us less for the four in the chain.

**The rivals.** Rival 2 needed PE at 1.2 GHz and long mutual blocking. Neither came. One of VectorE's adds met a pair of GpSimd's outputs:

```profile
1307.46 0.77 POOL L309 TENSOR_SCALAR y_sb<-y_sb,rstd_end,shift_end 128x512 f32<-128x512 f32 x1
1307.84 0.92 DVE L1383 SCALAR_TENSOR_TENSOR acc<-hinge,w2c,acc 128x512 f32<-128x512 f32 x1
1308.21 1.20 POOL L309 TENSOR_SCALAR y_sb<-y_sb,rstd_end,shift_end 128x512 f32<-128x512 f32 x1
```

The first output is undisturbed, the add takes 0.92 for 0.75 and ends 0.5 behind it, and the second output takes 1.20 for 0.77 and ends 0.65 behind the add: 0.6 us for that meeting. Together with the y of 127 above, 0.6 us of such stretching stands on the chain (0.17 and 0.39), near the one microsecond I took for all. By the rule of the Trainium skill (SBUF — State Buffer, the section on two separate sides) VectorE's two-input instruction and GpSimd's take turns, each waiting for the one that started first. The order of the three ends agrees with it, and so do three small instructions of GpSimd in the closing (0.49, 0.70 and 0.62 us for 0.19 or 0.20) that end 0.04 or 0.05 us behind an add of VectorE's. What I had too large was how often they would meet. Rival 3's ring of yT on ScalarE exists as a wait of 1.25 us once, and at 2.24 us where GpSimd folds; in the changed kernel it never set the pace. Rival 4 fell with C's 11.0. Rival 1, the full clock, was right about the clock and wrong about the sum (1326 for 1333.66).

**What stays open.** How the 10 us between the closing alone and the kernel with folds on GpSimd divide between the copy of yT (2 to 3 us) and the late start of y and outputs is an inference by subtraction. How the loop's part would do without the closing was not run either. What decides whether the clock falls behind the same waits, in five executions of nine behind the 2.12 us, and in one of two behind 1.52 and 1.98 us in the closing alone, no run here shows.

## What to carry to other kernels

A part of a schedule that is rewritten needs all its terms anew, the last one above all: when results that used to trickle come together, the queue that stores them becomes the chain, and a better order ahead of it is worth little until its issues are shared. When compute gets faster, count a ring for each transfer's place too (slots per place, less the time it is read, against the landing time), and look for memory that is free by then. An edit is worth what its neighbours let it be: here the loop's part gave 12.8 us with the closing in place, although A and B together are only 7.5 us shorter than before. And before a longer stretch is put down to an edit, look at the clock column: twice here, in A and in C, some 1.6 us came and went with it in the same program.

## What the runs showed of the hardware

- SP issues a store of 64 x 512 fp32 every 0.62 us, ScalarE's queue one every 0.66 to 0.76. With both in use, the stores of ScalarE's queue land after 3.3 to 3.6 us and SP's after 2.7 to 2.9; SP's alone after 2.4. In the last microseconds one queue moved 164 to 246 GB/s in each full slice of the DMA view, the two together 149 to 394, mostly over 220 (two tiles' stores from ScalarE's queue).
- TensorE's clock: in the changed kernel's closing, idle times up to 1.6 us, with PE busy for 66% of ten microseconds, left it at 2.4 GHz. It fell to 1.2 GHz behind waits of 2.73, 0.56, 1.95 and 1.39 us in twelve, and in one execution of two behind 1.52 and 1.98 us. Behind one wait of 2.12 us the next large product took 4.84 to 4.96 us in five executions and 3.60 in four.
- A 128x512 output on GpSimd takes 0.77 us, a 128x2 power 0.69 where a 128x1 power takes 0.55, and the other small instructions 0.19 us for one column and 0.19 to 0.20 for two: the second column of a pair costs 0.14 us or less.
- An instruction of VectorE's with two SBUF inputs and one of GpSimd's lengthen each other: an add 0.92 us for 0.75, an output 1.20 for 0.77. A y on VectorE, with one SBUF tensor as input, took 0.93 us for 0.54 beside an output of GpSimd's.
